# Attention on one core: two weight passes moved ahead of the query and key copies, and the squares of the projected rows moved between the next turn's first exponentials

## The reference

```
x = x + rmsnorm( softmax(rms(Q) rms(V)^T) V  Wo )        # attention: 16 query heads, 4 kv heads of 32
x = x + xattn(ctx, ctx, layernorm(x))                    # long convolution, computed with matrices
x = x + ffn(layernorm(x))                                # ternary weights, integer activations
```

## Time and profile before

| what | us |
|---|---|
| median of 3 runs | 661.15 |
| the runs | 660.64 to 663.03 |
| profiled execution, span of its instructions | 659.4 |
| attention, to the last copy | about 288.8 |
| one turn of the loop (exponential 0 to exponential 0) | 31.15 |

### The profile page before, as it was taken

The page is one execution under the profiler, slowest core; times in us unless marked ns, Lnnn a source line. Parts: engine busy times, 40 slices in busy tenths (PEclk is TensorE's granted clock), DMA queues, the critical chain, the costliest instruction groups (busy, mean ns, idle before and its releaser), DMA issues.

```text
span 659.4 us, 10218 instructions
## 1 busy us (share of the span) xinstructions
PE 585.6 (89%) x2590; PEld 326.3 (49%) x2590; DVE 484.5 (73%) x936; ACT 456.6 (69%) x783; POOL 363.4 (55%) x327
## 2 busy tenths in 40 slices
PE   6699889898989896979999999985699999999975
PEld 3344353535354442357777777762244444444332
DVE  2637768677777684437778778789789999989860
ACT  1264665757484856258888988874679888888961
POOL 1052616162534434547777777751677777777761
PEclk9899999999999996899999999996889999999997
DMA  8774254545464635036556656532135353443424
GB/s 295 234 229 104 57 125 164 127 159 129 164 152 156 170 109 131 25 87 184 174 158 194 169 166 184 182 92 81 32 66 111 96 121 96 107 96 83 96 70 105
DMA packets 87976, 87.08 MB, mean 132 GB/s; under 512 B 46288, under 2 KB 62160, under 8 KB 87824
## 3 DMA queue, kind: packets, MB, share of 16 engines
q1 hardware_dynamic: 87952, 86.81, 48.7%
HBM read 51.71 MB, written 4.28 MB: 85 GB/s over the span
## 4 chain that ended last, share of the span: by engine, by line
PE 26%; POOL 10%; DVE 8%; issue 7%; DMA 2%; ACT 1%; DVEq 0%; POOLq 0%; SPq 0%; ACTq 0%
PE ps L783 20%; POOL big L1410 5%; PE ps L1168 3%; POOL ys L1418 3%; PE ps L1153 2%; DVE toep L1295 2%; DMA act8t<-ys 1%; DVE st L1247 1%; POOL r L1406 1%; DVE qo L836 1%; POOL xq L1425 1%; DMA toep<-krows 1%; DVE mb L1299 1%; DVE ot L1333 1%; DVE ps L1262 1%
## 5 line engine op out<-in xcount | busy, mean ns | idle before, releaser
L783 PE MATMUL ps<-kv,toep 128*128 128x288 f32 x640 | 156.1, 407 | 1.9 <-PEq L1481 1.1
L783 PEld LDWEIGHTS ps<-kv,toep 128*128 128x128 f32 x640 | 120.9, 190 | 37.0 <-issue 4.2
L1168 PE MATMUL ps<-wt,xqt 128*128 128x512 bf16 x512 | 121.7, 389 | 13.3 <-DVE toep L1295 9.9
L715 POOL TENSOR_TENSOR pts<-big 128x512 f32<-128x512 f32 x64 | 85.2, 1340 | 56.8 <-ACT big L432 56.6
L432 ACT ACTIVATE big<-ps,kscale 128x512 f32<-128x512 f32 x128 | 85.8, 687 | 43.0 <-PE ps L273 40.3
L1410 POOL TENSOR_TENSOR big<-toep,wst 128x512 f32<-128x512 f32 x64 | 83.1, 1299 | 51.5 <-DVE toep L1295 50.9
L273 PE MATMUL ps<-qx,kx 128*128 128x512 f32 x128 | 77.6, 630 | 18.4 <-ACT big L432 12.1
L1168 PEld LDWEIGHTS ps<-wt,xqt 128*128 128x128 bf16 x512 | 49.8, 100 | 76.8 <-DVE toep L1295 12.8
L836 DVE TENSOR_REDUCE qo<-big 128x2048 f32 (+1 forms) x32 | 72.2, 2257 | 0.0
L592 DVE RECIPROCAL yt<-ps 128x256 f32<-128x256 f32 (+1 forms) x24 | 54.8, 2285 | 20.3 <-PE ps L293 20.3
L771 POOL TENSOR_TENSOR kv<-ctx 128x768 f32<-128x768 f32 (+1 forms) x32 | 52.5, 1642 | 30.3 <-PE ps L783 27.6
(11 more groups left out here) (127 smaller groups left out, 964.0 us busy)
## 6 DMA issues: line engine op xcount, KB each, us to landing
qx<-kv SPq DMA_DIRECT2D x128, 128.0 KB, 2.4
wst<-in_wall SPq DMA_DIRECT2D x12, 1024.0 KB, 6.8
wst<-in_wall SPq DMA_DIRECT2D x48, 256.0 KB, 3.7
toep<-krows SPq DMA_DIRECT2D x32, 256.0 KB, 3.7
ctx<-in_ctxt SPq DMA_DIRECT2D x32, 192.0 KB, 2.6
qo<-in_xt SPq DMA_DIRECT2D x8, 512.0 KB, 3.9
out_y<-ot SPq DMA_DIRECT2D x16, 256.0 KB, 2.2
conv_part<-qo SPq DMA_DIRECT2D x14, 256.0 KB, 2.9
```

Of the source, the lines that this page charges most:

```text
L715: nc.gpsimd.tensor_tensor(pts[:, n % 6, :], pt[:, 0, kv, gp * C:(gp + 1) * C], pt[:, 1, kv, gp * C:(gp + 1) * C], ALU.add).then_inc(s_ps.s ...
L783: mm = pe.matmul(m.ps[:, LB * r + lb, :].rearrange("p (b s) -> p b s", s=WIDE)[:, :, 0:PAIRS], m.toep[r][:, d * P:(d + 1) * P], m.kv[r][:, ...
L1168: mm = pe.matmul(bank[:, n % 2, :], xqt[r][:, k, :], wt[:, k, n * C:(n + 1) * C], start=(k == 0), stop=(k == CK - 1))
```

## The change

On ACT alone, the order of three things changes; no instruction is added or dropped.

- Weight pass 0 moves from the end of the turn to before `q_high`, and weight pass 1 to between `q_high` and `kx`.
- The squares of half 0 and half 1 of batch i - 1 leave the end of turn i - 1; in turn i half 0 stands behind exponential 0 and half 1 behind exponential 1. For the last batch they stay at the end.
- The wait of half 0 for the sums of the batch before goes.

```diff
-        def qk_out(i):
+        def qk_out(i, sums=False):
...
             q_high(0)
             q_high(1)
+            if sums:
+                weight_sums(i - 1, 1)
             for h in range(2):
                 wait(act, s_kt, i, h + 1)
...
         def turn(i, has_prev=True, has_next=True):
-            for n in range(3):
-                exponential(i, n)
+            exponential(i, 0)
+            if has_prev:
+                project(i - 1, 0)
+            exponential(i, 1)
+            if has_prev:
+                project(i - 1, 1)
+            exponential(i, 2)
...
             if has_prev:
                 q2_out(i - 1, 0)
+            if has_next and has_prev:
+                weight_sums(i, 0)
             if has_next:
-                qk_out(i + 1)
+                qk_out(i + 1, sums=has_prev)
             if has_prev:
                 q2_out(i - 1, 1)
-            if has_next and has_prev:
-                weight_sums(i)
-            project(i, has_prev)
```

More of the change, by code:

```diff
@@ L438, in q2_out, with project, weight_sums @@
                      TB[:, t, :].rearrange("p (k t) -> p k t", k=CK)).then_inc(s_q2e.sem, 1)
[L440 to L454, removed]
-        def turn(i, has_prev=True, has_next=True):
-            for n in range(3):
-                exponential(i, n)
+        def project(i, t):
+            wait(act, s_wo, i, t + 1)
+            if t == 1:
+                wait(act, s_sso, i, 1)
+            act.activation(osq, OB[:, t, :], ACT.Square, accum_out=sso[:, t:t + 1]
+                           ).then_inc(s_sso.sem, 1)
+        def weight_sums(i, r):
+            act.wait_ge(d_ws[r].sem, i * 16)
+            act.activation(wst[:, r, :], wst[:, r, :], ACT.Abs,
+                           accum_out=m.wabs[:, bass.ds((i - 1) * 2 + r, 1)]).then_inc(s_abs.sem, 1)
+        def turn(i, has_prev=True, has_next=True):
+            exponential(i, 0)
[5 more added lines that the diff above has]
+            exponential(i, 2)
             if has_next:
@@ L499, in _ @@
         turn(B - 1, has_next=False)
+        for t in range(TT):
+            project(B - 1, t)
         for t in range(TT):
```

## The result

The changed kernel takes 668.68 us (median of 4 runs, 668.01 to 669.98) against 661.25 for the kernel before on the same chip: a ratio of 1.0107, 95% interval 1.0089 to 1.0124. It is slower, and outside the range of 659.2 to 665.8. Run again beside the first experiments it took 666.83 (12 runs) against 662.06, ratio 1.0063 (1.0033 to 1.0092): the sign holds, the size is 7.4 us in the one comparison and 4.8 in the other. Ratios and intervals are taken over the fast executions alone and are not the quotients of the medians printed beside them.

The account below looks back on a forecast made before the run. No engine is full; a ring of waits through ACT, POOL's additions and PE's `sum_weights` bounds each turn. Ring 31.30 us against 31.15 and +0.60 in turn 1 add 1.6 to 661.15: 662.8 us, range 659.2 to 665.8.

Parts of the forecast that it names:

- the ring: Chain of waits setting a turn's length, through sums of squares, POOL's additions and `sum_weights`: 31.15 us now, 31.30 forecast.
- The passes hide: Both weight passes fit ACT's idle gaps before `q_high` and `kx`, about 1.0 and 1.2 us left; cost taken as 0.
- Exponential 0 about 0.84 us after score 0, the sums at v + 2.42: On ACT, exponential 0 starts at 124.30; sums of squares are ready at 126.74, 0.28 us later than now.
- that rival: ACT's accumulator reads may keep the next exponentials from overlapping: over 0.5% slower, in full 666.4 us; chance 0.10.
- POOL's arm takes over: PE waits some 1.8 us at `sum_weights` for POOL's additions, 9.47 us after the sums, replacing 1.72 before score 2.
- The ring of 31.30 us, +0.60 in turn 1: Each turn takes 2.42 + 9.47 + 19.41 = 31.30 us against 31.15; turn 1's `sum_weights` comes 0.60 later.
- the 1.6 us forecast: Turn 7's sums of squares come at 252.72 against 251.10 now, adding 1.6 us to the span.
- Turn 7's own way keeps its length: Turn 7's 9.23 us to `sum_weights` and all that follows it were taken as unchanged.
- My 1.8 is next to the harmless row, so the sum stays at 662.8: PE's new 1.8 us wait, nearer 1.72 (clock 1.00) than 2.75 (clock 0.54), adds no clock loss.
- the free wait: PE's some 1.8 us wait at `sum_weights` was taken to leave its clock, and the 662.8 us, unchanged.
- the third rival: PE's clock falls every loop turn, five turns each losing at least `sum_weights`' 0.88 us: 667.2 us; chance 0.05.
- The first rival: POOL does not hold `sum_weights`, so PE's 1.7 us comes through in turns 2 to 6: 652.6 us; chance 0.09.

Follow-up runs that it names:

- the first experiments: Earliest follow-up runs, one being the changed kernel with idle matmuls in PE's wait at `sum_weights`: 663.09 us, against 666.83 for the changed kernel beside it.
- the squares alone: Kernel before with only the squares moved between the next turn's exponentials, weight passes kept at the end of the turn: 671.48 us, ratio 1.0116.
- the squares later: Changed kernel with both squares one place later on ACT, behind exponentials 1 and 2: 671.63 us, ratio 1.0140.
- the passes alone: Kernel before with only the two weight passes moved as in the change, squares left at the end of the turn: 651.94 us, ratio 0.9831.
- the wait filled: Changed kernel with two idle float32 matmuls of 512 columns on PE ahead of `sum_weights`: 663.09 us, ratio 0.9987.
- the squares earlier: Changed kernel with both squares right behind exponential 0: 663.26 us, ratio 1.0006.
- the additions first: Changed kernel with POOL's power `rs4` moved behind addition 3: 656.63 us, ratio 0.9914.
- the last version: Kernel before with only the weight passes moved, plus idle 256-column matmuls on PE in turn 7: 650.11 us, ratio 0.9820.

## Why the prediction was wrong

It had the mechanism and the sign of each part of the ring right, and it failed in one step, on the clock: the wait that moves on PE was given no price.

- *The passes hide*: right. 1.08 and 1.33 us are left in turns 1 to 6, where I had 1.0 and 1.2.
- *Exponential 0 about 0.84 us after score 0, the sums at v + 2.42*: right. In turn 1 the score record starts at 63.23 and the exponential at 64.06 (0.83), the sums are ready at v + 2.39; nothing kept the handovers from overlapping, so that rival is out.
- *POOL's arm takes over*: right. The wait is named by the trace in all seven turns, 13.0 us in total, where before it was turn 7's 2.75 alone. `sum_weights` comes 9.43 to 9.46 us after the sums in turns 2 to 5, 9.35 and 9.25 in turns 1 and 6 (9.47 predicted).
- *The ring of 31.30 us, +0.60 in turn 1*: 31.21 to 31.25 where the clock held, +0.45 in turn 1. Up to turn 7's `sum_weights` the ring taken alone made 1.1 of the 1.6 us forecast.
- *Turn 7's own way keeps its length*: within chance. Its wait grew from 2.75 to 3.63 and 3.56 us, and the way from `sum_weights` to the first convolution went both ways, 21.33 and 18.52 us against 20.10.
- *"My 1.8 is next to the harmless row, so the sum stays at 662.8"*: wrong; this is the step that failed. I set a wait of 1.8 us beside one of 1.72 that had done no harm in five turns of one profile and one of 2.75 that seemed to, and let the distance between lengths decide. The rows do not carry that. The wait of 2.75 us begins at 257.58, and turn 7's clock was at its half level before it (kernel before, columns as in the earlier trace rows):

```profile
248.10:254.00 5.90, 2.81 (x8) 1.18 (x6) 1.96 (x4) 5.66 (x11) 1.99 (x2) 0.97 0.87 198
254.00:260.30 6.30, 3.47 (x5) 1.15 (x4) 4.37 (x8) 3.79 (x6) 4.83 (x5) 0.50 0.38 134
```

And length does not part harmless from harmful. The waits ahead of score 2 in the kernel before are 1.71 to 1.80 us; the longest, in turn 6, passed without a fall:

```profile
220.64 0.47 PE L273 MATMUL ps<-qx,kx 128*128 128x512 f32 x1 [1.80 <-ACT big L432]
```

The changed kernel's clock fell in turn 6 behind a shorter wait at `sum_weights`:

```profile
233.50 1.06 PE L293 MATMUL ps<-pts,ones 128*32 128x512 f32 x8 [1.75 <-POOL pts L719]
```

What the runs showed in place of the free wait: the new waits were mostly 1.75 to 2.05 us; in each of two profiles the clock fell in two of the five turns 2 to 6, and each fall cost 1.5 to 1.6 us, where I had priced 0.88 for the eight matmuls and nothing for the work behind them. In the first profile the falls in turns 2 and 6 (1.64 and 1.47 above the 31.23 of turns 3 to 5) are 3.1 of the 4.2 us between turn 1's v and turn 7's `sum_weights`; the ring is the other 1.1. Filling the wait took the falls away. The 667.2 of the third rival lies near what was measured, but by other terms: five falls of 0.88 there, two of 1.5 to 1.6 here. The rule of the Trainium skill, page "TensorE: Matmul & The Clock Gate", section "HAM oscillation — how this bites in real kernels", whose case I put at 0.05, names the pattern: idle gaps that come back each round, and work that starts cold behind them. The page's example has waits for DMA and a cold start in every round; here it was two rounds of five.

The first rival's 1.7 us per turn exist: 1.7 come through with the squares left at the projection, and some 1.3 with the additions ahead of `rs4`. The change as written blocks it, as forecast.

What stays open: why waits of 1.71 to 1.80 us ahead of score 2 brought no fall in the profile of the kernel before, and waits of 1.75 to 2.05 at `sum_weights` did in some turns. Place and what surrounds the wait differ together, and no run parts them. Nor is it shown that the kernel before is free of such falls: one execution of it was profiled, at a granted clock of 0.966 over the whole span, and of the 40 beside the experiments five took 665.9 to 668.6 us at 0.959 to 0.961.

## What to carry to other kernels

Where two waits meet, one of them released by each half of a change, ask which half lengthens the other's arm: here moving the passes freed 10 us and moving the squares closed the door on them, and only trying each half alone shows it. A reduction whose result a long chain waits for belongs directly behind what produces it, ahead of work that only fills a buffer. And a wait on TensorE that is moved, not removed, can have a price of its own: compare its clock over several turns and several executions, for one profile of one place says little about another.

## What the runs showed of the hardware

TensorE's granted clock fell to its half level in 7 of the 20 turns 2 to 6 of those four profiles in which PE stands at `sum_weights` for 1.7 to 2.6 us in most turns (the changed kernel twice, the squares alone, the squares later). It fell in none of the 25 turns of the five profiles where that wait is under 1 us or gone (the passes alone, the wait filled, the squares earlier, the additions first, the last version). A fall can show only after PE is at work again: in turn 2 of the changed kernel `sum_weights` still took 1.07 us and the q step 1.34 us later 1.79. With the squares later, behind a wait of 2.57 us, `sum_weights` itself took 1.94.

Two useless matmuls in the wait are cheaper than the falls: with them the same kernel was 3.7 us faster. In turn 7 the stretch from `sum_weights` to the first convolution took 17.35 us with them, where the changed kernel takes 21.33 or 18.52 and the kernel before 20.10; that part was not tried on the kernel before alone.
